# Unread products for TensorE in the stretches where it waits: a pre-norm decoder layer with routed experts on one core

## What is computed

```python
x = x + attn(_layernorm(x), g1, Wq, Wkv, Wout, g2)      # 16 heads of 64, one shared k and v, q and k l2-normed, causal
x = x + xattn(_layernorm(x), ctx, ctx, W_q, ..., b_out) # 16 heads of 16, 77 context rows
x = x + ffn(_layernorm(x), w_router, w_v, w_proj)       # argmax over 4 experts
# ffn:
expert_idx = argmax(softmax(x @ w_router))
gate_raw, value = split(x @ w_v[e]);  h = silu(gate_raw) * value;  y = h @ w_proj[e]
```

## Time and profile before

| | |
|---|---|
| three timed runs | 995.59, 996.25, 998.47 us; median 996.25 |
| the profiled execution | 1001.04 us, its span 999.3 us |
| mean granted TensorE clock in the span | 0.939 |
| busy: TensorE, VectorE, ScalarE, GpSimd | 88%, 61%, 56%, 20% |
| chain that ended last | TensorE 49%, VectorE 6%, issue 5%, GpSimd 3% |

### The profile page before, as it was taken

How to read it: one execution, slowest core, us unless ns; L and a number is a source line. 1 busy time by engine, 2 the same in 40 slices (tenths; PEclk the granted TensorE clock), 3 DMA queues, 4 the chain that set the end, 5 groups by cost and what they waited for, 6 DMA issues and landing times.

```text
span 999.3 us, 14240 instructions
## 1 busy us (share of the span) xinstructions
PE 882.3 (88%) x4366; PEld 669.0 (67%) x4366; DVE 612.9 (61%) x1417; ACT 562.5 (56%) x1112; POOL 203.9 (20%) x220
## 2 busy tenths in 40 slices
PE   4699898999999897999989999999760299999997
PEld 2467676777777675776776777777550178888885
DVE  4667758667858677668766778778766133323231
ACT  1478667677867577667758678768442022222221
POOL 3212321302112121212313020201103401111111
PEclk9699999999999999999989999999955599999999
DMA  8300000020000000000000003200232201010100
GB/s 283 71 1 1 1 1 1 1 85 1 1 2 0 1 2 0 2 1 0 2 1 1 1 1 107 63 1 1 85 127 72 81 1 32 20 32 21 32 17 9
DMA packets 19175, 29.01 MB, mean 29 GB/s; under 512 B 2079, under 2 KB 15648, under 8 KB 19104
## 3 DMA queue, kind: packets, MB, share of 16 engines
q1 hardware_dynamic: 17008, 22.73, 7.5%
q0 software_dynamic: 1680, 4.21, 1.2%
q10 hardware_dynamic: 416, 1.18, 0.3%
HBM read 21.41 MB, written 7.10 MB: 29 GB/s over the span
## 4 chain that ended last, share of the span: by engine, by line
PE 49%; DVE 6%; issue 5%; POOL 3%; ACT 2%; DMA 1%; DVEq 0%; ACTq 0%; POOLq 0%
PE W L1418 7%; PE S L1395 6%; PE O L1395 5%; PE O L1235 3%; PE O L1232 3%; PE S L1217 3%; PE S L1216 3%; PE O L1233 3%; PE W L1306 3%; PE W L1348 3%; PE W L1274 2%; PE W L1328 2%; POOL sorted_rows L700 2%; PE W L1336 1%; PE W L1361 1%
## 5 line engine op out<-in xcount | busy, mean ns | idle before, releaser
L944 DVE TENSOR_TENSOR pl<-pr,ph 128x512 fp32r<-128x512 f32 x288 | 200.2, 698 | 72.4 <-ACT pr L750 64.4
L749 ACT ACTIVATE ph<-S 128x512 fp32r<-128x512 f32 x288 | 173.7, 603 | 107.5 <-PE S L1217 105.2
L750 ACT ACTIVATE pr<-S 128x512 f32<-128x512 f32 x288 | 172.7, 600 | 0.0
L1232 PE MATMUL O<-ph,vhi 128*65 128x512 f32 x288 | 145.1, 504 | 0.0
L1235 PE MATMUL O<-pl,vhi 128*65 128x512 f32 x288 | 116.3, 404 | 8.2 <-DVE pl L944 7.8
L1217 PE MATMUL S<-qT,kT 128*128 128x512 f32 x288 | 115.3, 400 | 0.0
L1216 PE MATMUL S<-qT,kT 128*128 128x512 f32 x288 | 115.0, 399 | 0.0
L1233 PE MATMUL O<-ph,vlo 128*65 128x512 f32 x288 | 114.7, 398 | 0.0
L651 POOL TENSOR_TENSOR rs<-ri,half 128x1 f32<-128x1 f32 x48 | 34.9, 727 | 306.0 <-DVE ri L883 306.0
L1274 PE MATMUL W<-wqkv,zT 128*128 128x384 f32 x192 | 75.5, 527 | 3.8 <-DVE qT L996 1.6
L858 ACT ACTIVATE gate<-S 128x512 f32<-128x512 f32 x38 | 20.6, 596 | 102.8 <-PE S L1395 102.8
(11 more groups left out here) (174 smaller groups left out, 1637.8 us busy)
## 6 DMA issues: line engine op xcount, KB each, us to landing
raw<-in_w_v SPq DMA_DIRECT2D x16, 512.0 KB, 4.0
wps<-in_w_proj SPq DMA_DIRECT2D x4, 1024.0 KB, 10.1
sorted_rows<-pad_row SPq DMA_DIRECT2D x19, 128.5 KB, 4.3
xs<-sorted_rows SPq DMA_DIRECT2D x19, 128.5 KB, 2.0
wqkv<-in_wqkv_t ACTq DMA_DIRECT2D x1, 1152.0 KB, 6.3
wout<-in_wout_t SPq DMA_DIRECT2D x1, 1024.0 KB, 10.0
xall<-in_x SPq DMA_DIRECT2D x1, 1024.0 KB, 10.3
xall<-in_x SPq DMA_DIRECT2D x1, 768.0 KB, 7.8
```

What stands on the lines that cost most here:

```text
L749: nc.scalar.activation(ph[:, k % RING, :], S[k % AHEAD][:], ACT.Exp, scale=SIM_SCALE).then_inc(ph_ready, 1)
L750: nc.scalar.activation(pr[:, k % RING, :], S[k % AHEAD][:], ACT.Exp, scale=SIM_SCALE)\
L944: nc.vector.tensor_tensor(pl[:, k % RING, :], pr[:, k % RING, :], ph[:, k % RING, :].bitcast(F32), ALU.subtract).then_inc(pl_ready, 1)
L1232: nc.tensor.matmul(o, vhi[:, vs, 0:DH + 1], ph[:, k % RING, :], start=j == 0, stop=False)
```

## The change

TensorE gets products that nobody reads: 128 x 128 `ident` by 128 x 128 `ones`, float32, written to the first 128 columns of S[0]. They stand at twelve places: ahead of ten named side stages (a table gives the count for each), 22 of them behind the setting of `pe_done`, and 9 ahead of the first `turn_rows`. Ahead of stages of tiles 14 and 15 TensorE first waits until all exponentials of the attention steps are read (`p_ready` at 288), which frees S[0]; ahead of the nine it waits for `scattered`. No other engine's stream is touched, and no existing instruction of TensorE changes its place among the others.

```diff
+BUSY = {("z_turn", 0, 0): 9, ("q_turn", 0, 0): 12, ("z_turn", 0, 1): 5, ("out_proj", 0, 15): 5, ("xo_turn", 0, 14): 10,
+        ("scores", 3, 15): 4, ("probs_turn", 0, 15): 11, ("probs_v", 0, 15): 3, ("xo_turn", 0, 15): 1, ("xattn_out", 0, 15): 1}
+BUSY_ROUTING = 22
+BUSY_LAST = 9
...
+            def keep_busy(n):
+
+                for _ in range(n):
+                    nc.tensor.matmul(S[0][:, 0:P], ident[:], ones[:], start=True, stop=True)
+
...
+                    if (name, part, t) in BUSY:
+                        if t >= 2:
+                            pe.wait_ge(p_ready, N_STEPS)
+                        keep_busy(BUSY[name, part, t])
...
             pe.wait_ge(side_ready, N_SIDE)
             pe.sem_inc(pe_done, 1)
+            keep_busy(BUSY_ROUTING)
...
+            pe.wait_ge(scattered, 16 * TILES)
+            keep_busy(BUSY_LAST)
             turn_rows(0)
```

## The result

The changed kernel takes 986.36 us in the median of four runs (984.48 to 986.91), against 997.36 us of before (995.59 to 1004.11, the three runs shown above and a fourth). The ratio is 0.9874, 95% interval 0.9825 to 0.9923: 1.3% faster, and clear of the noise. The forecast was 988.0 with a range of 981 to 995. Later runs of both on one chip gave 986.85 against 997.89 us, ratio 0.9897 (0.9878 to 0.9916).

The account below looks back on a forecast made before the run. TensorE's chain, last to end for 49% of the span, was taken as the bound, slowed where its clock is low. First tiles 2.5, last tiles' chain 4.5 and feed forward 1.2 sum to 8.2 us: median 996.25 to 988.0, range 981 to 995.

Parts of the forecast that it names:

- When the clock moves: TensorE's clock rises only behind 3.6 to 5.9 us of unbroken work and falls in every wait from 3 us up.
- First tiles: Tiles 0 and 1: blocks raise and hold the clock so `qkv` runs faster; 2.5 us, between 0 and 6.
- the four chances in ten for an early rise: Clock up by 9.6 us, ahead of tile 0's `qkv`, after nine products: 0.4 x 3.4, that is 1.4 us.
- The even chance for tile 1's `qkv`: If the clock lasts through 25 to 30 us, tile 1's `qkv` takes 3.9 instead of 5.89 us: 0.5 x 2.0.
- Last tiles' chain: From `xo_turn` of tile 14 on, blocks restore full clock for tiles 14 and 15: 4.5 us, between 0 and 5.2.
- Feed forward: Nine products ahead of `turn_rows` raise the clock before `up`: 2.3 us at four to six chances in ten, 1.2 us.
- Routing: 22 products in the 6.93 us wait ahead of the counting products: cost nothing warm, give at most 0.3 us.
- (1): Only the last tiles' chain answers, 3.9 us blocks being too short: gain 1 to 4 us, 992.5 to 995; chance 0.17.
- (2): Everything answers and the clock outlasts VectorE's wait in the last tiles' chain: 13.4 us, 983; chance 0.10.
- (3): Products run at 1.2 GHz and overrun five of their waits: with nothing gained costs 6.1 us, 1002.3; chance 0.07.
- (4): At all places, unread products of two constants leave the clock alone and do not overrun: 996; chance 0.04.
- the rule on transposes: Trainium skill: PE-mode transposes do not count as busy for the clock; first tiles would then bring 1.5 us, not 2.5.

Follow-up runs that it names:

- the part alone: Kernel before plus only that place's blocks: first tiles 993.89 us, last tiles' chain 992.76, ahead of feed forward 995.06, each against 997.78.
- the first two part-kernels with the block: Kernel before plus only the first tiles' three blocks (993.89 against 997.78 us), or only nine products ahead of tile 0's `z_turn` (995.90 against 997.32).

## Why the prediction was right, point by point

- **What bounds, and where the clock is low.** Right: the gain came from the stretches that the page's clock row showed, and the chain's shares stayed.
- **The price of a product.** Right: 18 instructions in 3.88 us, nearly all at 1.2 GHz (3.9 forecast), 24 in 2.84 at 2.4 (2.6).
- **When the clock moves.** The readings here were too tidy, already for the trace of before. It had a rise that did not come behind unbroken work: at 733.6 us TensorE was idle, in the wait of 1.52 us behind the three `scores`, so the clock did not outlast that wait but came up in it. And it had unbroken work without a rise: the 4.47 us of `probs_v` from 742.39 us, at 1.2 GHz from end to end. "It falls in every wait of 3 us and more" holds for that trace and not for all others. The wait of 3.02 us near 330 us was outlasted in nine of 14 traces, and step 0's wait of 3.30 us, where nothing fills it, in two of twelve. The fall behind `qn` was at 23.6 us (0.79 in the row of 23 to 24), not at 23.8, and the page has three low slices behind 725 us and one at the start, not four and two. None of these readings is a term of the sum, but they are what its chances were taken from.
- **First tiles.** The mechanism was right, the chances too low. The term was 2.5 us between 0 and 6 (its sum writes 0.4 for a term of 0.5 and takes 2.5 for 2.8); the part alone gave 3.9 in the median, and 5.65 and 5.55 in the two traces with nine products in which all went well. The step that was mis-sized is the four chances in ten for an early rise: it happened in five of seven traces. I had asked that the clock be up at 9.6 us, when `z_turn` starts, but a rise at 10.1 or 10.4 us, as in the traces of the first two part-kernels with the block, still comes before `qkv`. The work right behind a block belongs to it. The even chance for tile 1's `qkv` was about fair: with blocks at these three places it took 4.11 us in four traces (in two of them the clock had risen late) and 5.80 in two.
- **Last tiles' chain.** The 3.1 us wait and the fall came as told (3.24 us). Up to `probs_v` the chain saved 1.28 us (1.1 forecast), on `probs_v` 2.06 (2.05). But `xo_turn` and `xattn_out` saved 0.13 instead of 1.35 us: "the clock is up again" was right for `probs_v` alone, and it fell behind it, at 735.6 us. The chain's shift at VectorE was 1.0 us, not 1.35, as GpSimd's root (721.24) took 1.46 us beside VectorE's `weights_low` of 1.22, where it takes 0.55 elsewhere in this chain, and VectorE stood idle for it for 0.44 us. In sum 3.47 against 4.5 us in the trace, and 5.0 in the median of the part alone.
- **Feed forward.** The same misjudgement as at the start: 1.2 us stood for four to six chances in ten at 2.3 us; in seven of eight traces the clock was up for `up`, and the part alone gave 2.7 us, 2.1 in the table above. Block, `turn_rows` and the short wait behind it together were enough.
- **Routing.** Right in that nothing was measured; the traces show 0.5 us in the counting products where 0.3 at most was forecast.
- **Rivals.** That only the chain answers (1) is refuted by the two parts outside it, 3.9 and 2.7 us. That the clock outlasts VectorE's wait as well (2) did not happen: it fell. Overrun (3) is real (8.1 us for twice the products at three places) but its condition did not come about: every block that could hold up the chain was at 2.4 GHz or rose inside. Products that leave the clock alone (4), and the rule on transposes, are refuted.
- **The sum.** 8.2 us were forecast and 11.0 measured in the medians; 988.0 came as near to 986.36 as it did because the three runs that the forecast started from had a median 1.1 us under that of all four. By the medians of the parts the misses were +1.4 (first tiles), +0.5 (chain) and +1.5 (feed forward). By the traces the chain missed by -1.0, so a gain that did not come, `xattn_out`'s, stood against two chances that were set too low. That the total fell well inside the range owes something to that.

## What to carry to other kernels

Where an engine with a granted clock waits a few microseconds for others on the chain, unread work in the wait pays what the work behind it costs at the lower clock, and only there: 22 products ahead of 30 us without work for TensorE gave nothing that the medians show, and a full clock on a stretch that VectorE paces gave 0.1 us. Size a block so that it ends before the wait does at the clock that it will have, since it can't be called off, and count the real work right behind it as a part of it. Judge such a change by medians and by parts: single traces here differ by 2 us in a stretch where nothing was changed, only because the clock fell in one wait or not.

## What the runs showed of the hardware that was not expected

- Float32 transposes raise and hold TensorE's clock like products: 18 transposes in 4.07 us ahead of `up`, rise at 782.6 us, and a ratio of 0.9908 against 0.9897.
- The moment of a rise is not fixed to the work. The same nine products from 5.2 us brought it at 8.6 to 10.4 us in five traces and at 14.3 and 14.4 us in two.
- The clock can fall while TensorE works, and rise while it waits. At 735.6 us in the changed kernel, at the end of `probs_v`, TensorE had waited 1.06 us and then worked since 733.29; at 733.6 us in before it rose in a wait of 1.52 us.
- The same wait brings the clock down in one execution and not in the next: the 3.02 us near 330 us did in five of 14 traces.
- GpSimd's root of one column took 1.46 or 1.47 us beside a VectorE subtraction of 1024 columns, in all nine traces of kernels with the blocks in the chain, and 0.55 us without, in the five others. That one holds up the other was not tested here.
